# One of 112 gather groups fetched row by row by SyncE instead of by GpSimd

## The reference, cut to what matters

```python
h = x @ W
norm = deg_inv_sqrt[src] * deg_inv_sqrt[dst]
msgs = h[src] * norm[:, None]
out = jax.ops.segment_sum(msgs, dst, num_segments=N)
```

```python
return jnp.einsum('blf,fd->bld', out, W_out) + b_out
```

## Time and profile before

| | |
|---|---|
| time before, median of 3 runs | 2533.95 us (2532.27 to 2534.63) |
| the profiled execution, its own time | 2532.77 us |
| span of its trace | 2531.0 us |
| PE busy over the span | 2180.2 us (86%) |
| POOL busy over the span | 1577.2 us (62%) |
| mean granted clock of TensorE | 0.914 of full speed |

### The profile page before, as it was taken

One profiled execution on the slowest core, in us unless ns is written; L12 is line 12 of the kernel. 1 busy time (PEld: TensorE's weight loads), 2 busy tenths in 40 slices (PEclk: granted clock), 3 DMA queues, 4 the chain that ended last, 5 costly groups with the idle time before them and its releaser, 6 DMA issues. The chain is left out here.

```text
span 2531.0 us, 45136 instructions
## 1 busy us (share of the span) xinstructions
PE 2180.2 (86%) x12457; PEld 1820.9 (72%) x12458; DVE 1437.1 (57%) x3727; ACT 821.5 (32%) x2306; POOL 1577.2 (62%) x2083
## 2 busy tenths in 40 slices
PE   6977777777777777768899999999989999995998
PEld 5745555555655555558799999767769999993998
DVE  9855544543554554548522222399978888886111
ACT  2512222221221111125233333255544444441333
POOL 4767777777777777740355555387757777760333
PEclk9988888888887888765999999999999999996999
DMA  5243333333333333342233343242221111111121
GB/s 171 81 115 106 106 105 106 105 106 106 105 106 105 105 106 105 105 125 88 72 117 109 119 134 107 84 116 86 87 67 44 46 48 50 46 46 59 34 38 30
DMA packets 138832, 227.46 MB, mean 90 GB/s; under 512 B 26861, under 2 KB 99234, under 8 KB 138738
## 3 DMA queue, kind: packets, MB, share of 16 engines
q0 software_dynamic: 56160, 142.61, 20.3%
q1 hardware_dynamic: 81058, 82.07, 9.8%
q10 hardware_dynamic: 1520, 1.58, 0.2%
HBM read 174.86 MB, written 51.30 MB: 89 GB/s over the span
## 5 line engine op out<-in xcount | busy, mean ns | idle before, releaser
L932 POOL DMA_INDIRECT all_XN<-h_table,l_srcI x782 | 739.7, 946 | 245.4 <-issue 237.9
L1136 PE MATMUL gcn_acc<-all_XN 128*128 128x256 f32 x780 | 239.3, 473 | 113.3 <-DMA all_XN<-h_table,l_srcI 113.2
L1136 PE MATMUL gcn_acc<-all_XN,gcn_hot 128*128 128x256 f32 x784 | 244.7, 479 | 91.0 <-DMA all_XN<-h_table,l_srcI 90.8
L1136 PEld LDWEIGHTS gcn_acc<-all_XN 128*128 128x128 f32 x780 | 183.1, 241 | 157.8 <-DMA all_XN<-h_table,l_srcI 124.4
L1136 PEld LDWEIGHTS gcn_acc<-all_XN,gcn_hot 128*128 128x128 f32 x784 | 187.0, 245 | 136.0 <-DMA all_XN<-h_table,l_srcI 101.2
L1831 ACT ACTIVATE moe_hidden<-moe_hid_ps,moe_b 128x128 f32<-128x128 f32 x420 | 131.2, 363 | 278.8 <-PE moe_hid_ps L1912 278.8
L1912 PEld LDWEIGHTS moe_hid_ps<-moe_xst,held_held 128*128 128x128 f32 x1680 | 202.8, 192 | 10.6 <-issue 6.0
L1912 PE MATMUL moe_hid_ps<-moe_xst,held_held 128*128 128x128 f32 x1680 | 206.1, 276 | 0.6 <-DVE moe_xst L1852 0.6
L1919 PE MATMUL moe_y_ps<-held_held,moe_hidden 128*128 128x256 f32 x840 | 199.1, 380 | 1.7 <-ACT moe_hidden L1831 1.0
L2556 PE MATMUL att_hid_ps<-att_xpt,held_held 128*128 128x128 f32 x1568 | 183.5, 275 | 0.0
L2556 PEld LDWEIGHTS att_hid_ps<-att_xpt,held_held 128*128 128x128 f32 x1568 | 179.5, 192 | 0.3 <-issue 0.2
(11 more groups left out here) (440 smaller groups left out, 4629.9 us busy)
## 6 DMA issues: line engine op xcount, KB each, us to landing
held_held<-in_e_w SPq DMA_DIRECT2D x32, 512.0 KB
slots_out<-moe_y SPq DMA_DIRECT2D x105, 128.0 KB
all_XN<-h_table,l_srcI POOLq DMA_INDIRECT x782
all_X<-in_x SPq DMA_DIRECT2D x7, 896.0 KB, 11.0
rows_table<-all_XN SPq DMA_DIRECT2D x7, 896.0 KB, 4.1
z_table<-held_held SPq DMA_DIRECT2D x49, 128.0 KB
x_table<-all_XN SPq DMA_DIRECT2D x49, 128.0 KB, 1.7
out<-all_X SPq DMA_DIRECT2D x49, 128.0 KB, 1.7
```

The lines of the kernel that those rows point to most:

```text
L932: nc.gpsimd.indirect_dma_start(msg[b][:, c, :], None, self.h_table, bass.IndirectOffsetOnAxis(self.srcI[:, GE * g + c:GE * g + c + 1], 0)) ...
L1136: last = nc.tensor.matmul(acc[b % NA][:, :], hot[b % NH][:, c, :], msg[b][:, c, :], start=(c == 0), stop=(c == n - 1))
```

## The change

Group 110, the last but one (`ROWED = G - LAG`), is no longer gathered by POOL. SP fetches its 7 x 128 = 896 rows one at a time: for each it loads the node's number from `srcI` into a register and issues a DMA of one row of 1 KB from `h_table` at that address, into `rowed`, a new piece of `XN`. Each of the seven tiles has a semaphore of its own, `rowed_in[c]`. PE waits for each tile's semaphore ahead of that tile's matmul. POOL skips the group. The attention's `xt[0]` moves from `XN` to a tile of its own, which makes room for `rowed`. The load of `b_out` moves from SP to ACT, behind ACT's loop over the keys and values.

```diff
-            xt = [piece.rearrange("p (b n) -> p b n", b=KB) for piece in (rest[:, taken + 2 * P + 1:taken + 2 * P + 1 + D], s.sb("xt1", [P, D])[:, :])]
-            taken += 2 * P + 1 + D
+            xt = [s.sb(f"xt{i}", [P, D])[:, :].rearrange("p (b n) -> p b n", b=KB) for i in range(2)]
+            taken += 2 * P + 1
+            ROWED = G - LAG
+            rowed = rest[:, taken:taken + GE * D].rearrange("p (c d) -> p c d", d=D)
+            taken += GE * D
...
+            rowed_in = s.sems("rowed_in", GE)
...
                     sp.wait_ge(w_in, 32)
-                    sp.wait_ge(ctx_ready, 1)
-                    sp.dma_start(b_out, io["l0_vecs"][0:1, :]).then_inc(b_in, 16)
-                    sp.wait_ge(b_in, 16)
+                    def rows_of_tile(c):
+                        col = GE * ROWED + c
+                        for p in range(P):
+                            node = sp.value_load(self.srcI[p:p + 1, col:col + 1], min_val=0, max_val=ROWS - 1)
+                            sp.dma_start(rowed[p:p + 1, c, :], self.h_table[ds(node, 1), :]).then_inc(rowed_in[c], 16)
+
+                    for c in range(GE):
+                        rows_of_tile(c)
+                    for c in range(GE):
+                        sp.wait_ge(rowed_in[c], 16 * P)
...
+                    act.wait_ge(ctx_ready, 1)
+                    nc.scalar.dma_start(b_out, io["l0_vecs"][0:1, :]).then_inc(b_in, 16)
                     act.wait_ge(xt_ready, T + 1)
...
                     for g in range(G):
+                        if g == ROWED:
+                            continue
...
                         n = edge_tiles(g)
-                        after(pe, msg_in[b], 16 * GE * q + 16 * n)
-                        if isinstance(g, int) and g < NP:
+                        rows = rowed if g == ROWED else msg[b]
+                        if g != ROWED:
+                            after(pe, msg_in[b], 16 * GE * q + 16 * n)
+                        if g < NP:
                             after(pe, hot_ready, g + 1)
                         for c in range(n):
-                            last = nc.tensor.matmul(acc[b % NA][:, :], hot[b % NH][:, c, :], msg[b][:, c, :], start=(c == 0), stop=(c == n - 1))
+                            if g == ROWED:
+                                pe.wait_ge(rowed_in[c], 16 * P)
+                            last = nc.tensor.matmul(acc[b % NA][:, :], hot[b % NH][:, c, :], rows[:, c, :], start=(c == 0), stop=(c == n - 1))
```

## The result

| | before | after |
|---|---|---|
| median of the runs, us | 2533.11 (2531.99 to 2534.63, 4 runs) | 2699.31 (2697.59 to 2700.07, 4 runs) |
| ratio, with its interval | | 1.0656 [1.0643, 1.067] |
| span of the profiled execution, us | 2531.0 | 2698.2 |
| mean granted clock | 0.914 | 0.889 |

The changed kernel is 166 us slower, where no measurable change was forecast (2531.8, range 2528.5 to 2545). On some of the later occasions the kernel before itself took 2686 to 2704 us, because POOL's gathers stall there (one chip gave 2704 us at one time and 2536 at another), so each run is compared with the kernel before that ran beside it alone.

A forecast was written before the change was run, and what follows sets the result against it. POOL's issue of gathers was taken to bound the gather stage, with PE's own chain setting its end. Only POOL's 2.1 us counted, all other parts 0: 2533.95 - 2.1 = 2531.8 us, range 2528.5 to 2545.

The forecast's parts named there:

- SP's part: SP's 896 row fetches beside POOL's gathers: 1.04 us a row, ending at 1073.6 us, 42 us ahead of PE, costing nothing.
- The gap of 44.5 ns: Time between two SP instructions, derived from a later stage; five gaps make 0.22 us of a row.
- The threshold: 1.084 us a row on SP, above which its last row misses PE's seventh tile of group 110, wanted at 1115.1 us.
- The second rival: SP's register load is slow directly behind a DMA: 1.27 us a row, 169 us late, 2701 us; chance 0.03.
- the main case: The whole kernel shows no change that can be measured: 2531.8 us, own range 2529 to 2537; chance 0.78.
- POOL's part: Seven gathers less at the gather stage's end save 2.1 us, not 8.8, because PE's own chain comes next.
- Plus or minus some half us: Uncertainty from the moving granted clock on the bounds, 0 and 2.13 us, of the saving at the gather stage's end.
- The zero terms: Costs taken as 0: SP's rows on the DMA engines, the bias load moved to ACT, and PE's seven waits.
- the rival of a slowed POOL: SP's stream slows POOL's gathers from 946 to 978 ns: 25 us on the path, 2557 us; chance 0.04.
- The bias on ACT: ACT issues the bias DMA, about 0.3 us, covered by idle time ahead of its copy of `xt`: cost 0.
- PE's seven waits: Seven semaphore waits in place of one ahead of group 110's matmuls: 0.3 us at most, taken as 0.
- The full 8.8 us appear: Rival: all seven gathers' time or more is saved, needing a shorter PE chain at the end: 2525.2 us; chance 0.05.

The follow-up runs named there:

- four_loads_on_time: The changed kernel with SP doing four register loads and then four DMAs, all 896 rows of group 110, no POOL stalls: 2530.64 us, 0.9978 of the kernel before.
- before_again: The kernel before, unchanged, run again for its profile while POOL's gathers stalled: 2702.61 us in one run.
- five_of_110_on_time: The changed kernel with SP fetching only tiles 0 to 4 of group 110, POOL gathering the other two, no stalls: 2531.08 us, 0.9978 of the kernel before.
- six_of_100_on_time: The changed kernel with SP fetching tiles 0 to 5 of group 100 instead, four loads then four DMAs, no stalls: 2528.83 us, 0.9969 of the kernel before.
- three_of_100: The changed kernel with SP fetching only tiles 0 to 2 of group 100, four loads then four DMAs: 2529.07 us, 0.9981 of the kernel before.
- fixed_rows: The changed kernel without SP's register loads and address arithmetic, its 896 DMAs fetching table rows 0 to 895: 2698.9 us, 0.9995 of the kernel before.

## Why the prediction was wrong, point by point

**SP's part is the step that failed.** "So a row costs 1.02 to 1.06 us. I take 1.04" should have been 1.273. Its term for the load, "the register load 268 ns", measured 489, which is 0.22 of the 0.23 us. The row was read where two other instructions stand between a DMA and the load; they hide 0.20 us of a time that the change lays bare. The other terms: arithmetic 152 for 159, check 18 for 31, address 37 for 46, DMA 278 for 293 to 332, together 0.06 us less, with 0.313 taken for the DMA. A sixth instruction, a MOVE of 29 ns between the address and the DMA, was left out, with its gap some 0.07 more. It could have been seen: the view of L1726 of before has it beside the two rows:

```profile
L1726 SPq MOVE slots_out<-moe_y x105: 29/29/35, 1237.5 to 1631.4; - x105
```

The gap of 44.5 ns was right: 489 + 152 + 18 + 37 + 29 + 278 = 1003 ns, and (1273 - 1003) / 6 = 45.

**The threshold fits.** PE wanted the seventh tile at 1111.94 + 12 x 0.236 = 1114.8 us, where 1115.1 was said. At 1.073 us a row four_loads_on_time just made it, with its last DMA at 1107.1; at 1.273 the change did not. "From 1.084 on all of it is on the path" fits on both sides; nothing was tried between them.

**The second rival happened, and its price was right by luck.** "The register load is slow directly behind a DMA" gave 1.27 us a row, the last row landed at 1284 us and 2701 us in all; measured were 1.273, the last DMA issued at 1284.1 with PE going on at 1285.4, and 2699.3. It had a chance of 0.03. The place was right, the closeness was luck. Its 483 ns come from the first load of the earlier trace rows, which does not stand behind a DMA: in the trace SP's last DMA ahead of it is 36 us earlier, and ACT's first load at the same place takes 482. And its row leaves out the MOVE with its gap (0.07 us), which its other instructions, together 0.08 too long, make up for. The evidence against it was "the load of the later stage, two short instructions behind a DMA, shows no trace of such a wait". That sentence took a duration for a wait: the wait is there, and partly hidden by the two instructions, as before_again shows. The trace of before could not decide between the two, since SP has no load directly behind a DMA in it; a chance much nearer that of the main case would have been right.

The Trainium skill's floor of about 600 ns for such a load ("DMA: Bandwidth & Descriptors", Latency and other measured facts) had spoken for trouble, and its direction was right here. Its size was not: 489 ns behind a DMA, 272 behind another load, and 2804 us would have been 105 too much.

**POOL's part: right in mechanism, its size in part open.** The last but one group's gathers do not save 8.8 us. The stall of 2.13 goes, and then PE's chain sets the end: five_of_110_on_time and four_loads_on_time both show 24 records in a row. Yet they saved 5.3 and 5.7 us, and the intervals (3.3 to 7.9 us less) leave out 2.1. From the start of sum 110 to the end of sum 111 it was 1110.87 to 1122.02, 11.15 us, and is now 5.38. Of these 5.8 us the stall is 2.1; the other 3.6 are the granted clock, 1.00 now against 0.66 and 0.72 before (windows of before from 1111 to 1116 and from 1116 to 1122 us):

```profile
1111.00:1116.00 5.00, 4.78 (x15) 3.52 (x13) 2.88 (x7) 0.45 (x1) 3.62 (x4) 0.66 0.33 100
1116.00:1122.00 6.00, 4.09 (x10) 3.00 (x10) 0.81 (x2) 0.00 (x0) 0.00 (x0) 0.72 0.09 22
```

"Plus or minus some half us, because the granted clock moves" was too narrow by several times. Nor does the clock follow from the missing stall: six_of_100_on_time has the stall and a clock of 1.00, three_of_100 has it and 0.72. It differs between executions of one kernel. The ten records of sum 110 that took 2.36 us in the change took 3.89 when it ran again, and in before_again the kernel before itself sums both groups in 5.38:

```profile
1111.68 3.89 PE L1155 MATMUL gcn_acc<-all_XN 128*128 128x256 f32 x10
```

```profile
1287.32 5.38 PE L1136 MATMUL gcn_acc<-all_XN 128*128 128x256 f32 x24
```

So these 3.6 us belong to the executions that are compared here. They can't be put down to the change, and what makes the medians 3 us better than the stall alone is open.

**The zero terms held.** In the change the gathers stay at 946 ns with the DMAs of SP beside them, so the rival of a slowed POOL is refuted; fixed_rows shows it for the DMAs apart, within its interval. The bias on ACT and PE's seven waits show in no wait of the profiles. "The full 8.8 us appear" did not happen for group 110; for group 100 the times fit a full 1.25 us for each gather.

## What to carry to other kernels

Price an instruction from a row in which the same instruction stands ahead of it, and sum a loop over every instruction that the trace shows for such a statement, not over those that its source suggests; when the margin over the threshold is 4%, the one step whose neighbour is new decides. A register load behind a DMA on SP is best put behind other loads: four loads and then four DMAs made a row 0.20 us shorter and turned 1.066 into 0.998. And work taken off an engine that bounds a stage should come from the middle of its sequence, where three and six pieces saved 4.9 and 7.5 us (their full time within the noise), not from an end at which another engine's chain is next.

## What the runs showed of the hardware

A register load on SP ends 0.46 to 0.57 us behind the end of the DMA issue ahead of it, at the median, with nothing, one or two short instructions between; counted from that issue's start it is 0.80 to 0.83 us in all four cases. In before_again it ended at the same distance whether it took 90 or 273 ns. Behind another load it takes 269 to 273 ns. The partition makes no difference (481 and 489 ns). What the load waits for in the DMA was not tried. A DMA of one 1 KB row takes SP 278 ns when it alternates with loads; of four in a row the first takes 278 at the median and the others 237 to 238. At times SP's and POOL's queues stall in the gather stage: the kernel before goes from 2534 to 2686 or 2704 us, the changed orders with 896 rows on SP go to 3150 to 3270; the waits are released by nothing in the program, and their cause stays open.
